# Sample loads of a gathered-expert kernel: one per sample on GpSimd's queue, stores on SyncE's, and a unit's column preparation spread over three chunks

## The reference

```python
s0 = relu(x @ swi[0]) @ swo[0]            # two shared networks, all samples
s1 = relu(x @ swi[1]) @ swo[1]
eo = relu(x @ wi[type]) @ wo[type]        # the sample's own expert
w  = softmax(relu(concat(eo[:,0], s0[:,0], s1[:,0]) @ g1) @ g2)
x  = x + eo*w[0] + s0*w[1] + s1*w[2]      # one w per sample
lap_x, lap_y = ...                        # second differences along columns and rows, reflected at the edges
out = x + zX*lap_x + zY*lap_y + zR*x*(1-x)
```

## Time and profile before

| | |
|---|---|
| median of three runs | 1206.76 us |
| the profiled execution's own time | 1203.73 us |
| its span | 1202.2 us |
| mean granted TensorE clock | 0.977 |
| TensorE matmul busy | 1143.8 us, 95% of the span |
| VectorE busy | 690.6 us, 57% |
| ScalarE busy | 451.1 us, 38% |
| GpSimd busy | 141.2 us, 12% |
| unit passes 3 to 23, by the first hidden low parts of pass 3 and pass 24 | 53.88 to 470.60 us |

### The profile page before, as it was taken

How to read it: one execution, slowest core, us unless ns; L and a number is a source line. 1 busy time by engine, 2 the same in 40 slices (tenths; PEclk the granted TensorE clock), 3 DMA queues, 4 the chain that set the end, 5 groups by cost and what they waited for, 6 DMA issues and landing times.

```text
span 1202.2 us, 17512 instructions
## 1 busy us (share of the span) xinstructions
PE 1143.8 (95%) x5872; PEld 969.2 (81%) x5872; DVE 690.6 (57%) x1032; ACT 451.1 (38%) x783; POOL 141.2 (12%) x243
## 2 busy tenths in 40 slices
PE   8998999879998989999999999999999999999995
PEld 7786887667887778888888888888888888888884
DVE  6755666455656654555655656556556556556564
ACT  2644554344454443233233223233233233233232
POOL 1123233212433231000000000000000000000001
PEclk9999999888999989999999999999999999999998
DMA  7555565544665451311311311211211221220200
GB/s 235 157 135 131 151 178 147 142 99 125 171 180 138 120 168 32 102 23 58 79 27 58 76 29 60 71 30 60 71 39 50 72 44 45 70 68 22 71 27 27
DMA packets 172906, 107.86 MB, mean 90 GB/s; under 512 B 143408, under 2 KB 152080, under 8 KB 172816
## 3 DMA queue, kind: packets, MB, share of 16 engines
q1 hardware_dynamic: 155328, 51.93, 18.3%
q0 software_dynamic: 17024, 54.54, 15.3%
q10 hardware_dynamic: 464, 0.26, 0.1%
HBM read 85.20 MB, written 17.04 MB: 85 GB/s over the span
## 4 chain that ended last, share of the span: by engine, by line
PE 64%; SPq 28%; issue 5%; DMA 1%; DVE 1%; ACT 0%; DVEq 0%; POOL 0%; ACTq 0%; POOLq 0%
SPq L1053 24%; PE acc L808 21%; PE acc L809 11%; PE hbank L783 11%; PE hbank L784 11%; PE hbank L785 10%; SPq L1028 3%; SPq L1029 0%; DMA xs<-in_x 0%; DMA rw<-in_L_cond_wi 0%; PE acc L715 0%; DMA y<-y 0%; PE tbank L746 0%; PE acc L797 0%; PE hbank L763 0%
## 5 line engine op out<-in xcount | busy, mean ns | idle before, releaser
L549 DVE SCALAR_TENSOR_TENSOR hl<-hbank,hh 128x512 fp32r<-128x512 f32 (+2 forms) x432 | 273.6, 636 | 456.7 <-ACT hh L873 456.2
L873 ACT ACTIVATE hh<-hbank 128x512 fp32r<-128x512 f32 (+2 forms) x432 | 237.3, 553 | 593.0 <-PE hbank L785 590.7
L808 PE MATMUL acc<-swo,hh 128*128 128x512 f32 x1024 | 370.9, 396 | 0.0
L809 PE MATMUL acc<-swo,hl 128*128 128x256 f32 x1024 | 286.8, 280 | 0.0
L808 PE MATMUL acc<-ewo,hh 128*128 128x512 f32 x528 | 202.9, 413 | 38.0 <-DVE hl L549 32.7
L808 PEld LDWEIGHTS acc<-swo,hh 128*128 128x128 f32 x1024 | 192.4, 188 | 45.3 <-DVE eo L567 0.2
L783 PE MATMUL hbank<-xh,swh 128*128 128x512 f32 x512 | 202.6, 396 | 0.0
L784 PE MATMUL hbank<-xl,swh 128*128 128x512 f32 x512 | 202.3, 395 | 0.0
L809 PEld LDWEIGHTS acc<-swo,hl 128*128 128x128 f32 x1024 | 193.1, 189 | 9.9
L785 PE MATMUL hbank<-xh,swl 128*128 128x512 f32 x512 | 199.2, 389 | 0.0
L808 PEld LDWEIGHTS acc<-ewo,hh 128*128 128x128 f32 x528 | 102.5, 194 | 64.3 <-DVE hl L549 36.5
(11 more groups left out here) (166 smaller groups left out, 962.9 us busy)
## 6 DMA issues: line engine op xcount, KB each, us to landing
rw<-in_L_cond_wi POOLq DMA_DIRECT2D x44, 512.0 KB, 4.3
rw<-in_L_cond_wo POOLq DMA_DIRECT2D x44, 512.0 KB, 5.0
xs<-in_x SPq DMA_DIRECT2D x16, 512.0 KB, 4.3
rw<-in_x SPq DMA_DIRECT2D x256, 32.0 KB, 2.2
ei<-eo_scratch SPq DMA_DIRECT2D x16, 512.0 KB, 5.6
eo_scratch<-eo POOLq DMA_DIRECT2D x120, 64.0 KB, 2.4
out<-ot SPq DMA_DIRECT2D x15, 512.0 KB, 6.3
xs<-in_x SPq DMA_DIRECT2D x464, 16.0 KB, 2.7
```

What stands on the lines that cost most here:

```text
L549: e.scalar_tensor_tensor(HL[:, g % NH, 0:w], bank[:, 0:w], 0.0, HH[:, g % NH, 0:w].bitcast(F32), ALU.max, ALU.subtract).then_inc(h_lo, 1)
L808: e.matmul(acc[j][:, 0:2 * D], HH[:, g % NH, js], woc[:, c, :], start=(c == 0), stop=False)
L809: m = e.matmul(acc[j][:, D:2 * D], HL[:, g % NH, js], woc[:, c, 0:D], start=False, stop=last)
L873: e.activation(HH[:, g % NH, 0:w], hbank[g % HRING][:, 0:w], ACT.Relu).then_inc(h_hi, 1)
```

## The change

The block loads of tiles 3 and up move from SyncE's queue to GpSimd's and become one DMA of 64 KB for a sample, with a semaphore pair of their own. They stand behind the four pieces of the unit before, which are no longer split by stores. The stores move to SyncE's queue; GpSimd keeps the second half of the last unit's. SyncE starts `load_tile_x(0)` and `load_tile_blocks(0)` ahead of the stores of units 19 and 20. The turn, the high part and the low part of the next unit's columns stand in chunks 2, 3 and 4 of a pass, and in chunks 0, 3 and 5 of a tiny unit's pass, all behind the hidden values of their chunk. The cuts of a unit's weights are all made in the pass before it, except pieces 1 and 3 of a unit that follows a tiny one.

```diff
-    if c != (3 if n < FIRST - 1 else 4) or n < 3 or n >= NP - 2 or (n >= FIRST and PASSES[n][1] % 2 == 0):
+def next_tile(n, c, step=0):
+    if n < 3 or n >= NP - 2 or (n >= FIRST and PASSES[n][1] % 2 == 0):
         return None
-    return tile_of(n) + 1
+    at = (4, 4, 5) if n >= FIRST - 1 else (0, 3, 5) if UNITS[n - 2][1] == 2 else (2, 3, 4)
+    return tile_of(n) + 1 if c == at[step] else None
 ...
 def cuts_at(n, c):
     out = list(FIRST_CUTS.get((n, c), ()))
+    if 3 <= n <= 1 + NU and UNITS[n - 3][1] == 2 and c in (0, 2):
+        out.append((n, 1 + c))
     if 2 <= n < 1 + NU:
-        size = UNITS[n - 2][1]
-        late = 3 <= n and UNITS[n - 3][1] == 2
-        at = {2: 0} if size == 2 else {2: 0, 4: 2} if size == 4 else {3 if late else 2: 0, 5 if late else 4: 2,
-                                                                      6 if late else 5: 1, 7: 3}
+        at = {2: 0, 5: 2} if UNITS[n - 2][1] == 2 else {2: 0, 4: 2, 5: 1, 7: 3}
         if c in at:
             out.append((n + 1, at[c]))
-    if 3 <= n <= 1 + NU:
-        at = {2: {0: 2, 1: 1, 2: 3}, 4: {0: 1, 1: 3}, 8: {}}[UNITS[n - 3][1]]
-        if c in at:
-            out.append((n, at[c]))
     return out
 ...
             def turn_tile(tile):
 ...
-                    e.wait_ge(x_in[tile % 2], X_VAL[tile])
+                    e.wait_ge(xu_in[tile % 2], XU_VAL[tile])
 ...
+            def tile_steps(n, c):                       # VectorE
+                if next_tile(n, c) is not None:
+                    turn_tile(next_tile(n, c))
+                if next_tile(n, c, 2) is not None:
+                    tile_low_whole(next_tile(n, c, 2))
 ...
-                    if next_tile(n, c) is not None:
-                        turn_tile(next_tile(n, c))
-                    if next_tile(n, c - 1) is not None:
-                        tile_low_whole(next_tile(n, c - 1))
+                    if n >= FIRST - 1:
+                        tile_steps(n, c)
                 ...                                     # hidden_low(g), evacuate
                 if g < G:
+                    if n < FIRST - 1:
+                        tile_steps(n, c)
                     for ws, p in low_parts_at(n, c):
                         cut_low(ws, p)
 ...
-                    if next_tile(n, c) is not None:     # ScalarE
-                        tile_high_whole(next_tile(n, c))
+                    if n >= FIRST - 1 and next_tile(n, c, 1) is not None:
+                        tile_high_whole(next_tile(n, c, 1))
                 ...                                     # hidden_high(g), evacuate
                 if g < G:
+                    if n < FIRST - 1 and next_tile(n, c, 1) is not None:
+                        tile_high_whole(next_tile(n, c, 1))
                     for ws, p in cuts_at(n, c):
                         cut_high(ws, p)
 ...
+            def load_blocks(u):                         # GpSimd
+                tile = 1 + u
+                s0, k = slots_of(u)
+                if tile <= 4:
+                    e.wait_ge(t_prod, T_AT[tile - 2, 1])
+                else:
+                    e.wait_ge(xz_done, XZ_AT[tile - 2])
+                to = XS[tile % 2][:].rearrange("p j d -> p (j d)")[:, 0:128 * k] \
+                    .rearrange("p (c b n) -> p c b n", c=4, b=k)
+                for b in range(k):
+                    e.reg_load(regs[b % 4], tab[0:1, 0, s0 + b:s0 + b + 1])
+                    v = e.snap(regs[b % 4], min_val=0, max_val=NS - 1)
+                    rows = x[bass.ds(v, 1), :, :].rearrange("a r (k q n) -> q (a r k) n", k=2, q=4)
+                    e.dma_start(to[:, :, b, :], rows).then_inc(xu_in[tile % 2], 16)
+            for u in range(1, NU):
+                load_unit(u, (0, 2, 1, 3))
+                if u + 1 < NU:
+                    load_blocks(u + 1)
 ...
-            for u in range(1, NU):
-                load_unit(u, (0, 2))
-                if u >= 3:
-                    store_unit(u - 3)
-                load_unit(u, (1, 3))
 ...
-                    rows = sample.rearrange("a (r g) (k d) -> (a r) (g k) d", g=2, k=2)     # SyncE
-                    for q in range(4):
-                        qs = slice(32 * q, 32 * q + 32)
-                        e.dma_start(to[qs, :, b, :], rows[:, :, qs]).then_inc(x_in[tile % 2], 16)
 ...
-            for u in range(NU):
-                if u + 2 < NU:
-                    load_unit_x(u + 2)
-                elif u + 2 == NU:
+            for u in range(NU - 1):
+                if u == NU - 3:
                     load_tile_x(0)
-                if u == NU - 1:
+                if u == NU - 2:
                     load_tile_blocks(0)
-            store_last()
+                store_unit(u)
+            store_unit(NU - 1, 2)
```

More of the change, by code:

```diff
@@ L263, in cond_resid_program @@
         x_in = [sem(f"x_in{i}") for i in range(2)]
+        xu_in = [sem(f"xu_in{i}") for i in range(2)]
         eo_out = [sem(f"eo_out{i}") for i in range(2)]
@@ L340, in cond_resid_program @@
         for tile in range(1 + NU + NT):
-            x_slot[tile % 2] += 16 * (slots_of(tile - 1)[1] * (1 if tile <= 2 else 4) if 1 <= tile <= NU else 1)
+            x_slot[tile % 2] += 16 * (slots_of(tile - 1)[1] if 1 <= tile <= 2 else 0 if 3 <= tile <= NU else 1)
             X_VAL[tile] = x_slot[tile % 2]
+        u_slot = [0, 0]
+        XU_VAL = {}
+        for tile in range(3, 1 + NU):
+            u_slot[tile % 2] += 16 * slots_of(tile - 1)[1]
+            XU_VAL[tile] = u_slot[tile % 2]
         def stores(u):
@@ L992, in _ @@
             load_unit(0, (3,))
-            targets = [e.alloc_register(f"target{k}") for k in range(4)]
-            def store_unit(u, part=1):
+            regs = [e.alloc_register(f"row{k}") for k in range(4)]
+            def load_blocks(u):
+                tile = 1 + u
                 s0, k = slots_of(u)
-                e.wait_ge(acc_free, ACC[2 + u, blocks(2 + u) - 1])
-                for i, (b, g) in enumerate(stores(u)[::part]):
-                    e.reg_load(targets[i % 4], tab[0:1, 1, s0 + b:s0 + b + 1])
-                    v = e.snap(targets[i % 4], min_val=0, max_val=NS + NSLOT - 1)
-                    to, of = store_ends(u, b, g, v)
-                    e.dma_start(to, of).then_inc(eo_out[u % 2], 16)
@@ L1004, in _ @@
-            e.wait_ge(dve_seq, AT["targets"])
-            for u in range(1, NU):
-                load_unit(u, (0, 2))
-                if u >= 3:
-                    store_unit(u - 3)
-                load_unit(u, (1, 3))
-            store_unit(NU - 3)
-            store_unit(NU - 2)
-            store_unit(NU - 1, 2)
+                if tile <= 4:
[4 more added lines that the diff above has]
+                    .rearrange("p (c b n) -> p c b n", c=4, b=k)
@@ L1015, in _ @@
+            u = NU - 1
+            s0, k = slots_of(u)
+            e.wait_ge(dve_seq, AT["targets"])
+            e.wait_ge(acc_free, ACC[2 + u, blocks(2 + u) - 1])
+            for i, (b, g) in enumerate(stores(u)[1::2]):
+                e.reg_load(regs[i % 4], tab[0:1, 1, s0 + b:s0 + b + 1])
+                v = e.snap(regs[i % 4], min_val=0, max_val=NS + NSLOT - 1)
+                to, of = store_ends(u, b, g, v)
+                e.dma_start(to, of).then_inc(last_out, 16)
             t = NT - 1
@@ L1036, in load_unit_x, with store_unit @@
                     e.wait_ge(x_in[1], X_VAL[1])
[L1037 to L1041 removed]
                 for b in part or range(k):
                     v = table_value(0, s0 + b, b % 4, NS - 1)
[L1044 to L1057 removed]
+                    ps, js = unit_rows(u, b, 0)
+                    e.dma_start(XS[tile % 2][ps, js, :],
+                                x[bass.ds(v, 1), :, :].rearrange("a (r g) d -> (a r) g d", g=2)) \
+                        .then_inc(x_in[tile % 2], 16)
+            def store_unit(u, part=1):
                 s0, k = slots_of(u)
                 e.wait_ge(acc_free, ACC[2 + u, blocks(2 + u) - 1])
[L1060 removed]
+                for i, (b, g) in enumerate(stores(u)[::part]):
                     v = table_value(1, s0 + b, i % 4, NS + NSLOT - 1)
                     to, of = store_ends(u, b, g, v)
[L1063 removed]
+                    e.dma_start(to, of).then_inc(eo_out[u % 2], 16)
             def load_tile_x(t):
```

16 lines of the change are left out of this document (removed).

## The result

The changed kernel is slower: median 1228.5 us (four runs, 1223.1 to 1229.4) against 1205.7 (the three runs of before and a fourth, 1199.9 to 1207.7), a ratio of 1.019 with an interval of 1.014 to 1.024. The prediction was 1154 us, with 1186 as its upper end. The profiled execution took 1229.4 us, its span 1227.9.

The account below looks back on a forecast made before the run. SyncE's full DMA queue was taken as the bound. Idles of 24.5 + 11.1 less 2 gave 33.6 us, the clock 16, together 50 us off 1203.7: 1154 us, range 1144 to 1186.

Parts of the forecast that it names:

- SyncE's issue was the pace: Unit passes: SyncE's 464 DMAs, 3.44 us a sample, set the pace; late columns made 24.5 us of idles.
- The failed step: GpSimd's queue, big unit: 1.27 us a block load, last sample landed about 15 us behind the fourth weight piece before.
- Rival 2: Short passes: samples at 1.8 to 2.8 us, or queue order, make columns or weights late; 1165 to 1190 us; chance 0.17.
- The 4 us by which piece 0 was to be late: Behind eight samples in a tiny pass: next unit's piece 0 late about 4 us, for VectorE and ScalarE to absorb.
- Rival 1: GpSimd's queue becomes the pace from 3.1 us a sample; 1252 us at 3.5; chance 0.08 slower, 0.04 about as now.
- The two-port rule: GpSimd's loads beside VectorE copies: about 3.1 us a sample would cancel the gain; the rows spoke against it.
- The spread schedule: Tiny units' passes: spreading turn, low part and cuts removes 11.1 us of TensorE idle; small passes cost at most 6 us.
- Clock: Unit passes: an average of 0.95 cost 20.8 us of full-speed time; 16 us were taken as coming back.
- Stores in SyncE's queue cost nothing: SyncE's queue: 132 stores at 0.86 us, 117 us of issue against 399 us, so the queue is no longer full.

Follow-up runs that it names:

- e3: Kernel before with the new schedule and one 64 KB load per sample in SyncE's queue, stores left with GpSimd: 1145.1 us, 0.953.
- e5: Changed kernel with each looked-up sample's 512 runs of 128 bytes read 128 rows outermost, blocks in wrong places: 1145.8 us, 0.952.
- e8: Changed kernel with 512 scattered runs of 128 bytes from two fixed samples, rows outermost, wrong x: 1145.8 us, 0.955.
- e7: Changed kernel with half a unit's samples behind weight pieces 0 and 2, half behind 1 and 3: 1148.9 us, 0.955.
- e3b: Kernel before, old schedule kept, with one 64 KB load per sample in SyncE's queue and stores with GpSimd: 1172.7 us, 0.975.
- e1: Kernel before with only the new schedule of turn, high and low part and weight cuts: 1199.4 us, 0.998.
- e2: Changed kernel with the old schedule, so only the queue half of the change: 1239.2 us, 1.031.
- e4: Changed kernel with each sample loaded as 128 runs of 512 bytes, columns in wrong places: 1145.9 us, 0.953.
- e9: Changed kernel without the eighth sample's load in each of the eleven big units: 1171.4 us, 0.976.
- e11: Changed kernel with its block loads moved to SyncE's queue, unit u + 2 ahead of the stores of u: 1235.2 us, 1.029.

## Why the prediction was wrong, step by step

**SyncE's issue was the pace: right.** e3 leaves all else of this queue as it was, sends one load for four, and gains 57 us against its own before.

**The failed step: "At 1.27 us a big unit takes 10.2 us to issue, and the last sample lands within 2.7 to 5.0".** It put the load beside a `wo` piece for its 512 runs. Measured: 1.56 us in the engine; seven for 10.9 us, 5.9 us of standing still, 1.56 for the eighth, 18.4 us in all; the last landing 21.3 us behind the first issue, where the text had 13 to 15. Three terms were mis-sized. The engine's 0.77 was 1.56; e5 and e8 show 0.75 for 512 runs with rows outermost, so the `wo` row was the right price for the number of runs and the wrong one for the pattern. The landing, 2.7 to 5.0, was 6.1 and up to 9.4. The wait ahead of the eighth load had no term at all: the sum went by the engine's time alone and let eight loads go out without a stop. No row of before shows such a pattern, but the text said "the nearest in size of the pattern" where only the number of runs had been compared, and rows and order had not.

**What 2.3 us a sample means for the weights: also wrong.** Rival 2 stood for 1.8 to 2.8 us a sample and gave 1165 to 1190 us: big passes on time, short ones not. (Its own terms, 15 to 25 us kept back from 1154, give 1169 to 1179.) Measured are 18.4 / 8 = 2.3 us and 1229. Its place was right, since nine of TensorE's eleven idles are in short passes, but its size was not: it let part of the old idles stay, where they grew from 38.1 to 46.3 us and the clock fell as well. It counted columns (8 x 2.2 + 5 = 23 us) against a pass of 22.3 and left out that the next unit's three pieces stand behind these eight. 18.4 us of loads and four pieces of 0.77 are 21.5 us of line in a pass of 22.3 us, with the pieces at the end of it. e7 shows it: same load, same queue, other order, 1149 us. The 4 us by which piece 0 was to be late, "which VectorE and ScalarE have to absorb with two chunks in hand", were 64.5 us of ScalarE in eleven waits, of up to 11.4 us. Either error put right is enough: e5 and e8 change the price of the load alone, e7 the order alone, and all three stand at 0.952 to 0.955.

**Rival 1 named the right mechanism with a wrong threshold.** It had GpSimd's queue take SyncE's place and decide from 3.1 us a sample, the queue's share over all unit passes. That share was not reached: 181.0 + 65.4 = 246.4 us are 2.1 us a sample, and the engine still waited 67.9 + 42.4 = 110.3 us for free weight buffers. A queue need not be full to be the bound. It is enough that a burst stands ahead of something with a near due time. Its chance of 0.08 was for a full queue; a burst in one pass should have had a rival of its own.

**The two-port rule** of the Trainium skill (SBUF — State Buffer, "SBUF: two separate sides") would have made a load an estimated 3.1 us beside a VectorE copy. This case's trace does not show it: all 116 took 1558 to 1597 ns with VectorE busy 240.0 of 441.1 us; the rows of before had spoken against it and so do these. The higher price has another cause.

**The spread schedule: right, but only behind columns in time.** The text took 11.1 us of idles as gone and a share of the clock. e3 against e3b gives some 27 us, idles of 17.0 and clock of 0.97 to 1.00 (11.6 us). While columns are late it is worth 3 us (e1), or 11 to 15 us in the company of the new queues (e2 against the changed kernel: 1239.2 - 1228.5 by the medians, 1.031 - 1.019 by the ratios).

**Clock: right.** Where TensorE does not idle the clock stays at the upper level (e3, e7, e8: 1.00). In the changed kernel new idles brought new drops: 0.90, 23 us more than before.

**Stores in SyncE's queue cost nothing: right for time.** e4, e5 and e8 have them there at 1145.8 to 1145.9, e3 has them with GpSimd at 1145.1. In the changed kernel they landed in 4.6 us, and nobody waited for them. (The text's 117 us of issue for 132 stores should read 114; nothing hangs on it.)

With e8's price for a load the kernel takes 1146 us, and 1154 is within 1% of it. What was wrong was not the reading of the kernel before, but the price of an instruction that it did not contain, and the order in which a burst of them stood.

By the Trainium skill (DMA: Bandwidth & Descriptors, "Why a DMA increments its semaphore by 16 and not by 1") a DMA is split over as many engines, up to 16, as divide the outermost dimension of both of its patterns: four for quarters, 16 for 128 rows. On GpSimd's queue the runs agree in direction: 1.4 to 2.0 us a sample and a DMA share of 0.77 with four outermost, 0.55 with 128. On SyncE's queue the share with four outermost is 0.60 (e3), which the rule alone does not explain. Which engines moved a load is in no row here, so this explanation is not shown. The change to be had from it, the rows outermost with every 128 bytes at the place where the turn wants them, was not tried: the destination then needs the quarter ahead of the row in its partitions.

**Still open:** what fills up after seven such loads. The eighth starts when the seventh has landed, not when the first has. It is not bound to a unit: in e7 four loads from 104.77 and three from 112.52 are followed by a wait of 2.0 us, and in e9 seven from 193.16 by one of 2.2 us ahead of the next seven. With rows outermost eight in a row do not wait. A plain limit on loads in flight fits badly: when the eighth of pass 3 was due, at 69.6, three of the seven had landed, and it still waited for the other four. Room in the queue for packets, of which such a load has 80 and the others 32, would fit and is not shown. Units of five or six samples, or loads of twice the runs, would tell more.

## What to carry to other kernels

Price a DMA that the trace does not contain by its pattern and not by its bytes or runs: above all by what stands outermost in the source (the destination of every 64 KB load had its 128 partitions outermost). Take two prices for it, the issue in the engine and the rate at which the queue drains, and let the slower one set the length of a burst. When work moves into a queue, add up the burst that stands ahead of each thing with a due time; the queue's average share says little. When a long burst and urgent small transfers must share a line, halve the burst before buying a cheaper load: here the order alone took the ratio from 1.019 to 0.955, where 0.953 was to be had. And when a queue is full, first make its own instructions fewer in place; that (e3) was the fastest version that computes the same.

## What was not expected of the hardware

- A block load of 64 KB in 512 runs of 128 bytes: 1558 to 1597 ns of GpSimd's engine with four quarters outermost, 747 to 758 with 128 rows outermost, 535 to 553 as 128 runs of 512 bytes.
- The load with quarters outermost moves at 1.8 to 2.2 us a sample from SyncE's queue (14.2 to 17.8 us for eight, e11) and drains at 1.4 to 2.0 us from GpSimd's (in pass 3, 10.7 us for six). On GpSimd's queue it is 80 packets, the load with rows outermost 32.
- After seven such loads in a row GpSimd's next one stands 4.7 to 7.1 us and starts 0.3 to 0.6 us after the last of them has landed, in all eleven big units.
- In e5 the steps between loads are 0.92 us with a table read each, in e8, without one, 0.74; with the 1.56 us load the reads cost nothing, seven loads taking 10.91 us.
